# A selective scan whose odd states are weighed on TensorE by a diagonal of C instead of on ScalarE

## The reference

```
def step(h, inp):
    d_t, u_t, B_t, C_t = inp
    dA = jnp.exp(d_t[..., None] * A)
    h = dA * h + (d_t * u_t)[..., None] * B_t[:, None, :]
    y = jnp.einsum('bdn,bn->bd', h, C_t)
    return (h, y)
...
y = (ys + us * D[None, None, :]) * _silu(zs)
out = jnp.einsum('md,lbd->lbm', out_proj_w, y)
```

## Time and profile before

| | before |
|---|---|
| median of 3 executions | 545.38 us |
| profiled execution | 543.67 us |
| its span, first to last instruction | 541.5 us |
| TensorE matmuls busy | 434.6 us (80%) |
| VectorE busy | 397.5 us (73%) |
| ScalarE busy | 312.8 us (58%) |
| GpSimd busy | 216.0 us (40%) |
| mean granted TensorE clock | 0.914 |

### The profile page before, as it was taken

The page is one execution under the profiler, slowest core; times in us unless marked ns, Lnnn a source line. Parts: engine busy times, 40 slices in busy tenths (PEclk is TensorE's granted clock), DMA queues, the critical chain, the costliest instruction groups (busy, mean ns, idle before and its releaser), DMA issues.

```text
span 541.5 us, 9797 instructions
## 1 busy us (share of the span) xinstructions
PE 434.6 (80%) x3248; PEld 358.3 (66%) x3248; DVE 397.5 (73%) x722; ACT 312.8 (58%) x719; POOL 216.0 (40%) x157
## 2 busy tenths in 40 slices
PE   4989901938688585867999999999999999998733
PEld 2435601817567474756888988888988888897612
DVE  0878695996999999997564677777767777676453
ACT  2558975777999978987143453534355353435410
POOL 2300019693977979780323222223222222322010
PEclk9999975787896978889999999999999999999875
DMA  8942427141111223123000000000000000000000
GB/s 305 370 197 79 156 80 293 36 99 39 41 39 31 80 61 104 54 74 121 21 1 1 11 2 21 0 0 19 0 19 0 19 0 0 19 0 21 0 10 10
DMA packets 18793, 32.91 MB, mean 61 GB/s; under 512 B 2128, under 2 KB 11728, under 8 KB 17936
## 3 DMA queue, kind: packets, MB, share of 16 engines
q1 hardware_dynamic: 18768, 32.59, 17.9%
HBM read 26.26 MB, written 6.32 MB: 60 GB/s over the span
## 4 chain that ended last, share of the span: by engine, by line
PE 39%; issue 19%; DVE 14%; ACT 14%; DMA 7%; POOL 6%; SPq 1%; DVEq 1%; POOLq 0%; ACTq 0%
PE ps L396 31%; PE ps L507 5%; DMA ud_t<-ud_dram 5%; ACT hc L798 3%; POOL reg_b L1012 2%; ACT ps L790 2%; PE ps L604 2%; DVE ps L1172 2%; POOL reg_b L989 2%; DVE reg_b L1179 2%; POOL small L994 2%; ACT reg_b L773 2%; ACT reg_b L885 1%; DVE reg_b L1232 1%; DMA Nw<-x_fm 1%
## 5 line engine op out<-in xcount | busy, mean ns | idle before, releaser
L989 POOL TENSOR_TENSOR reg_b<-reg_c,reg_a 128x1024 f32<-128x1024 f32 x56 | 130.4, 2372 | 58.2 <-DVE reg_c L1123 57.9
L1012 POOL TENSOR_TENSOR reg_b<-reg_b 128x768 f32<-128x768 f32 x32 | 58.0, 1811 | 140.2 <-DVE reg_b L1232 107.6
L798 ACT ACTIVATE hc<-reg_b,bc 128x512 f32<-128x512 f32 x112 | 79.8, 713 | 25.0 <-PE ps L507 22.4
L396 PE MATMUL ps<-x1T,Mw 128*128 (+1 forms) x768 | 93.6, 278 | 0.6 <-ACT Mw L851 0.6
L396 PEld LDWEIGHTS ps<-x1T,Mw 128*128 128x128 f32 x768 | 88.2, 192 | 4.3 <-ACT Mw L851 0.9
L507 PE MATMUL ps<-ident,hc 128*128 128x128 f32 x452 | 75.3, 315 | 16.0 <-ACT hc L798 15.8
L1179 DVE SCALAR_TENSOR_TENSOR reg_b<-reg_c,bc,ps 128x512 f32<-128x512 f32 x112 | 81.8, 736 | 0.0
L507 PEld LDWEIGHTS ps<-ident,hc 128*128 128x128 f32 x452 | 61.2, 163 | 27.2 <-ACT hc L798 26.3
L1172 DVE TENSOR_TENSOR ps<-ps,reg_b 128x512 f32<-128x512 f32 x96 | 65.7, 690 | 8.8 <-ACT ps L790 8.7
L885 ACT ACTIVATE reg_b<-ps,small 128x128 f32<-128x128 f32 x128 | 45.3, 365 | 39.1 <-DVE small L1237 38.4
L790 ACT ACTIVATE ps<-reg_b 128x512 f32<-128x512 f32 x112 | 65.4, 585 | 4.1 <-POOL reg_b L989 4.1
(11 more groups left out here) (138 smaller groups left out, 698.3 us busy)
## 6 DMA issues: line engine op xcount, KB each, us to landing
reg_a<-a_dram SPq DMA_DIRECT2D x4, 1024.0 KB, 7.8
Mw<-w_o SPq DMA_DIRECT2D x1, 2048.0 KB, 16.0
ud_dram<-reg_b SPq DMA_DIRECT2D x4, 512.0 KB, 3.7
zs_dram<-x1T SPq DMA_DIRECT2D x4, 512.0 KB, 3.7
Nw<-zeros SPq DMA_DIRECT2D x1, 2048.0 KB, 9.8
mring<-w_q SPq DMA_DIRECT2D x8, 256.0 KB, 2.9
ud_t<-ud_dram SPq DMA_DIRECT2D x8, 256.0 KB, 3.5
zs_t<-zs_dram SPq DMA_DIRECT2D x8, 256.0 KB, 2.6
```

The source lines that it names most:

```text
L396: return pe.matmul(o, l, r, start=start, stop=stop)
L798: act.activation(hc[:, (n + 1) % WRING, :], H[:, n, :], ACT.Copy, scale=bc[:, t, s:s + 1]).then_inc(hc_s, 1)
L989: pool.tensor_tensor(dA[:, g % RING], delta_r[:, bass.ds(t, 1), :].to_broadcast([P, SA, DI]), Abc[:, g * SA:(g + 1) * SA, :], ALU.mult).th ...
L1012: pool.tensor_tensor(rq[:, g % 2].rearrange("p a c n -> p (a c n)"), pc[:, g % 2].rearrange("p a c n -> p (a c n)"), psn[:, g % 2].rearran ...
```

## The change

In time steps 1 to 7, the odd states are weighed on another engine. ScalarE multiplies the 128x128 identity by the state's column of C, which gives a diagonal matrix, and writes it to the first 128 columns of the slot of `hc`. TensorE multiplies each of the four 128-column blocks of the state by this diagonal (`state_product`), a true fp32 product without the transpose flag, and adds it to `Y`: the product of the block, as the stationary operand, with a diagonal is the weighed and transposed block. The even states go as before. ScalarE no longer waits for an odd state to be written; TensorE does. VectorE may overwrite an odd state when TensorE has summed it a time step earlier, and waits for `y_s` instead of `hc_s`.

```diff
+            def state_product(t, n, slot, count, last_state):
+
+                pe.wait_ge(hc_s, count)
+                pe.wait_ge(h_s, NST * (t - 1) + n + 1)
+                for c in range(CI):
+                    last = pe.matmul(Y[:, c * P:(c + 1) * P], H[:, n, c * P:(c + 1) * P], hc[:, slot, 0:P],
+                                     start=False, stop=last_state, skip_group_check=True)
+                last.then_inc(y_s, 1)
+
...
                 for n in range(NST):
-                    state_sum((n + 1) % WRING, NST * (t - 1) + n + 2, n == NST - 1)
+                    if n % 2:
+                        state_product(t, n, (n + 1) % WRING, NST * (t - 1) + n + 2, n == NST - 1)
+                    else:
+                        state_sum((n + 1) % WRING, NST * (t - 1) + n + 2, n == NST - 1)
...
             def weigh(t, n):
 
-                act.wait_ge(h_s, NST * (t - 1) + n + 1)
                 need(act, y_s, NST * (t - 1) + n + 2 - WRING)
                 s = NST + n
+                if n % 2:
+                    act.activation(hc[:, (n + 1) % WRING, 0:P], ident[:, :], ACT.Copy,
+                                   scale=bc[:, t, s:s + 1]).then_inc(hc_s, 1)
+                    return
+                act.wait_ge(h_s, NST * (t - 1) + n + 1)
                 act.activation(hc[:, (n + 1) % WRING, :], H[:, n, :], ACT.Copy,
                                scale=bc[:, t, s:s + 1]).then_inc(hc_s, 1)
...
                 if not (isinstance(t, int) and t == 1):
-                    dve.wait_ge(hc_s, NST * (t - 2) + n + 2)
+                    dve.wait_ge(y_s if n % 2 else hc_s, NST * (t - 2) + n + 2)
```

## The result

The changed kernel took 549.92 us (median of 7 runs, 549.06 to 552.81) against 545.38 for the kernel before (542.91 to 548.81, 7 runs), a ratio of 1.0103 [1.0067, 1.0139]. A repeat gave 1.0100 [1.0063, 1.0138]. It is some 5 us slower, above the half percent that can be told from no change. The forecast of 546.7 was 3.2 us too low; the time lies in the range, and the case that came is a small form of the slower rival.

A forecast was written before the change was run, and what follows sets the result against it. VectorE's two passes per state were taken to bound each scan step at 22.0 us; shifts of the steps summed to +1.3 us on the median 545.38, giving 546.7 us, range 542.3 to 551.5 for 8 in 10.

The forecast's parts named there:

- the slower rival: In the scan, TensorE becomes the ring all follow: 1.05 us per product, W 20.3 us, +8 us, 553 us; chance 30%.
- same: Whole kernel: the forecast of 546.7 us and "it does nothing" (545.4 us) taken together, 542.7 to 548.1 us; chance 53%.
- W: TensorE's time in a scan step from `skip_sum` to its last side job: 18.75 us forecast, 18.41 before in step 5.
- Step 1: First scan step, with longer side jobs of 0.93 us: 19.8 to 20.4 us against 19.67 before, +0.5 us.
- Step 2: Second scan step: VectorE waits longer for the exponential of the 12th state, +0.6 us.
- Step 3: Scan: the 0.63 us wait on ScalarE goes, 0.2 us waits at state 12 come; -0.2 us with step 4.
- the loop: Scan: last side job releases the `ud_t` load, TensorE sums, ScalarE's `hc` ring waits, VectorE waits; four of five exponential waits.
- Step 4: Scan: W 18.0 us in place of 18.94, since TensorE idles little ahead and the clock can still be up; -0.9 us.
- Steps 5 and 6: Scan: period W + 4.5 = 23.25 us against 23.04 and 23.16 before; +0.2 and +0.1 us.
- Last step: Step 7 of the scan: W 18.75 us against 17.53, no VectorE time hides it before the projection; +1.2 us.
- Nearly all of the relief is worth nothing: Scan: ScalarE gives back 18 us, hidden by VectorE; gains only the 0.63 us wait and possibly an earlier last state.
- The faster one: Rival in the scan: TensorE's clock up sooner or always, W 16.4 us, -3.6 us, 541.8 us; chance 17%.

The follow-up runs named there:

- padded traces: Idle fp32 products added between scan and projection: kernel before with 12, 546.90 us, with 6, 544.95 us; changed kernel with 6, 550.52 us.
- relief only: Changed kernel, narrow weighting kept, odd states summed unweighed by transposes instead of products (output not the layer's): 544.57 us, ratio 1.0012.
- early load: Load of `ud_t` issued ahead of loads that wait for the last side job: changed kernel 538.29 us (0.9882), kernel before 538.94 us (0.9875).

## Why the prediction was right or wrong

**The case.** I had "same" at 53% and slower at 30%; it was slower. The scan gave +2.6 in the first pair and +2.9 in the mean of two pairs, against +1.3 in my sum. With the padded traces it is +3.6. The rest, some 1.5 to 2.5 of the 5 us, lies for the most part behind the scan, where I had written that the part "is untouched". That is true of its instructions and wrong of its time.

**Prices of the pieces: right.** Product 0.89 us (I had 0.93), at the low clock 1.71 (1.86), diagonal 0.392 (0.39). The low clock after a late load was 2 x (1 - 0.66) x 4.12 = 2.8 us in step 5 and 4.6 in the last, against my 4.7:

```profile
193.28:197.40 4.12, 4.12 (x25) 4.12 (x26) 3.52 (x7) 1.98 (x4) 4.12 (x2) 0.66 0.18 58
239.26:244.60 5.34, 5.34 (x28) 5.34 (x29) 4.32 (x8) 2.86 (x6) 4.12 (x2) 0.57 0.10 38
```

**W: right in number, by luck in part.** Forecast 18.75 us; measured 211.75 - 193.28 = 18.47 in step 5, 18.28 in the last (257.54 - 239.26; before 17.53). In step 5 the clock was low for only 2.8 us, and for that my working gives 18.75 - (4.7 - 2.8)/2 = 17.8. It had TensorE at work without a pause up to the last side job. In its last stretch TensorE waits for ScalarE, which has no gap there: from the third side job of step 5 to its last it is busy for all 3.95 us. In the last step, with no exponentials left, the same stretch takes 2.89 us, against 2.96 by my prices.

```profile
206.98:210.93 3.95, 3.60 (x27) 2.91 (x26) 3.95 (x7) 3.95 (x10) 3.95 (x2) 1.00 0.18 64
253.83:256.72 2.89, 2.89 (x27) 2.89 (x25) 1.29 (x2) 1.82 (x5) 0.00 (x0) 1.00 0.96 376
```

**Step 1: +0.5 said, +1.2 measured.** The first step's W was 116.14 - 94.82 = 21.32 us, against my 19.8 to 20.4 and 19.67 before. This is a term mis-sized, and not at the head: the first side job starts 103.16 - 94.82 = 8.34 us in, and my working gives 8.4 for a clock that is low for 5.7 us, as it was here (0.65 over 8.18 us). The last stretch, from the side job at 111.11 to that at 115.06, takes 3.95 us where my prices add up to 3.23, and the two stretches between add 0.4.

**Step 2: +0.6 said, 0.0 measured** (21.70 us in both kernels), though its wait for the exponential is there as before (5.72 and 5.46 us). The +0.6 was for state 12 with the clock low for 4.7 us, and 0 for 3.2; it was low for 2 x (1 - 0.70) x 5.53 = 3.3 us.

**Step 3: -0.4 said, +1.23 measured.** (The sum says -0.2 for steps 3 and 4, and then takes `skip_sum` of step 4 as 0.5 + 0.6 - 0.4 = 0.7 late, since a wait at state 12 of step 4 moves nothing that the loop depends on.) This is the step of the prediction that failed. I followed two things behind TensorE's head, exponential 12 and the last side job, and missed a third: the statistics of the norm, which VectorE takes behind state 9 and which need `out_proj`, itself behind the products of states 1 and 3. It waits 0.68 us at 102.83, in step 1, and 0.47 at 154.12, in step 3, 1.4 us in three waits in all. State 12 adds 0.56 in step 3, and of the 0.63 that was to go 0.37 stayed: 0.47 + 0.56 - 0.26 = 0.8 of step 3's 1.2 us. That the head carries the cost is shown by the pair above: 161.35 without products 1 and 3, 163.4 with them, and 1.0011 against 1.0100 in the whole time. That it does so by these waits is read from the traces, and no run moves the statistics alone.

**Step 4: -0.9 said, -0.38 measured,** by its W: 18.0 said, 18.66 measured, 18.94 before. The clock was up at its start, as forecast (0.66 us for four at 170.17), and stayed up:

```profile
170.17:178.00 7.83, 7.83 (x61) 7.57 (x62) 7.81 (x13) 7.29 (x16) 4.24 (x2) 1.00 0.18 52
```

My working gives 16.4 us for a step with the clock up throughout. So here, too, 2.3 us of W are not TensorE's own work as I priced it; they come late in the step, where it waits for the other engines (from the second side job of step 4 to the third it is busy for 4.17 of 5.10 us).

**Steps 5 and 6: +0.2 and +0.1 said, -0.1 and -0.1 measured. Last step: +1.2 said, +0.76 measured**, for the reason given: nothing of VectorE hides it.

**"Nearly all of the relief is worth nothing": wrong for the scan.** It is worth 4.2 us there when the products aren't (in the median of the whole kernel nothing of it was left). I priced it from VectorE's waits that name ScalarE alone (0.63 us) and called the others TensorE's loop. But ScalarE's ring stands inside that loop: shorter weightings hand TensorE the states earlier, so its last side job comes earlier too (in relief only W of step 5 is 206.48 - 188.87 = 17.61 us, 18.41 before). In relief only, the gaps of steps 3 to 6 are 22.19 to 22.61 us against 22.77 to 23.49 before. The product takes that gain back and 2.9 us more. My sum for the scan was only 1.3 to 1.6 us off in the first pairs because two errors of opposite sign, the relief and the products each priced too low, nearly cancelled.

**The rivals.** The faster one did not come: its condition (the clock up all through) held in step 4 alone, and even there W was 18.66 us where it wanted 16.4. The slower one, TensorE becoming the ring that all follow, gave the sign but not its +8 (its terms add up to 8.9): the product took 0.89 us at the full clock where it wanted 1.05, and W was 18.3 to 18.8 from step 4 on where it wanted 20.3. That its ring is the right place is shown by the early load, which cuts it and with it two thirds of the scan's loss.

**Open.** Whether the changed kernel systematically meets the lower clock in the tail. Its tails were 289.38, 289.36 and (padded) 288.21 us, those of the kernel before 286.13, 288.41 and (padded) 287.79 and 285.96. The medians (5.5 us apart in the repeat, of which the scan holds 2.9 to 3.6) speak for a difference of some 2 us there. So do the single executions: of the 18 of the changed kernel none took less than 548.27 us, and the traced one of 549.8 us would have taken 546.5 with a tail of 286.1, while 28 of the kernel before ran from 540.02 to 549.01. So a tail as short as 286.1 us was hardly among them. What sets the clock there stays open, and no experiment switched it by itself. The start varies as well: in the repeat the first `skip_sum` of the changed kernel stood at 96.16 us, 1.3 later than in its first trace.

## What to carry to other kernels

Before pricing an engine's relief at its own late waits, ask whether it stands inside a loop that another engine closes; a gain there comes out under that engine's name. List all that hangs on the head of a step, not only the last consumer: two added products at the head cost 5.0 us of scan, six late ones 0.8. Compare whole times, not one traced part: the relief took 4.2 us off the scan and nothing off the kernel. And where a wait repeats at the same distance behind a load, move the load first: it was worth 1.2%, with no arithmetic changed.

## What the runs showed of the hardware

The part behind the scan, the same instructions in all fourteen traces, took 286.0 to 290.7 us, in step with a granted clock of 0.93 down to 0.64 in one window of 24 us; one kernel showed 0.93 and 0.79. In a comparison of 5 us a spread of 4.7 is as large as the effect, and a profile of one execution can't tell it from an effect of the edit. Nor does it look like chance alone: none of the twelve executions of relief only came near the 539.6 us that the shortest tail would give it.

The level at which TensorE starts after an idle stretch did not follow from the stretch alone. The kernel before was low after 1.64 us, the changed one full after 2.52 us (170.17). With the early load it was full after 2.13 us and low after 2.83 and 3.26:

```profile
118.17 0.66 PE L513 MATMUL ps<-ident,ud_t 128*128 128x128 f32 x4 [2.13 <-DVE yT L1209]
140.22 1.11 PE L513 MATMUL ps<-ident,ud_t 128*128 128x128 f32 x4 [2.83 <-DVE yT L1209]
230.03 1.11 PE L513 MATMUL ps<-ident,ud_t 128*128 128x128 f32 x4 [3.26 <-DVE yT L1209]
```

A true fp32 product of 128x128 by 128 columns costs twice a transpose of the same block: 0.89 against 0.44 us for four (202.12 to 203.01; 203.01 to 203.45, where the next side job starts).
